# Two-layer cross attention on one core: TensorE's order inside a unit

## What is computed

```python
# layer 0
a = layer_norm(ctx);  Q, K, V = x @ Wq.T, a @ Wk.T, a @ Wv.T
attn = softmax(Q K^T / 4);  x1 = x + tanh(gate) * (attn V) @ Wo.T
# layer 1
q = layer_norm(x1) @ q_w + q_b;  k, v = ctx @ k_w + k_b, ctx @ v_w + v_b
hidden = softmax(q k^T / 4) v @ cproj_w + cproj_b + x1
y = gelu(layer_norm(hidden) @ fc_w + fc_b) @ proj_w + proj_b
return hidden + y
```

## Time and profile before

| what | us |
|---|---|
| median of 3 runs | 1924.65 |
| lowest and highest | 1922.05, 1927.8 |
| the profiled execution, its own time | 1921.35 |
| its span in the trace | 1919.6 |
| TensorE matmul busy | 1795.8 (94%) |
| TensorE weight load busy | 1172.1 (61%) |
| VectorE busy | 1405.2 (73%) |
| ScalarE busy | 1247.4 (65%) |
| GpSimd busy | 484.8 (25%) |

### The profile page before, as it was taken

The page is one execution under the profiler, slowest core; times in us unless marked ns, Lnnn a source line. Parts: engine busy times, 40 slices in busy tenths (PEclk is TensorE's granted clock), DMA queues, the critical chain, the costliest instruction groups (busy, mean ns, idle before and its releaser), DMA issues.

```text
span 1919.6 us, 83118 instructions
## 1 busy us (share of the span) xinstructions
PE 1795.8 (94%) x37316; PEld 1172.1 (61%) x37316; DVE 1405.2 (73%) x2389; ACT 1247.4 (65%) x2271; POOL 484.8 (25%) x498
## 2 busy tenths in 40 slices
PE   6789999999999999999899998999999999999996
PEld 5346656666676657666576665766666565766653
DVE  4577787777778777787767877787777877788752
ACT  3057667776567665777666776677666766576773
POOL 2041024103341043411423123420334104311130
PEclk9699999999999999999999999999999999999998
DMA  7534344252413533143431534325251353324200
GB/s 183 98 86 114 99 127 98 85 137 61 127 46 92 129 101 94 55 107 98 126 87 48 129 95 119 77 77 147 64 128 45 92 129 101 95 50 122 48 3 12
DMA packets 149785, 178.88 MB, mean 93 GB/s; under 512 B 35860, under 2 KB 113853, under 8 KB 149429
## 3 DMA queue, kind: packets, MB, share of 16 engines
q1 hardware_dynamic: 147285, 170.67, 34.5%
q10 hardware_dynamic: 2144, 2.90, 0.6%
HBM read 125.33 MB, written 48.16 MB: 90 GB/s over the span
## 4 chain that ended last, share of the span: by engine, by line
PE 68%; DVE 17%; DMA 5%; ACT 4%; POOL 2%; issue 2%; SPq 2%; ACTq 0%; POOLq 0%
PE p_misc L1186 23%; PE p_mx L1186 14%; PE p_sc L1186 14%; PE p_acc L1235 13%; DVE maxes L921 8%; PE p_misc L1256 3%; DVE rest L1001 3%; ACT parts L764 2%; DMA scr_max<-max_rows 2%; DVE parts L1012 1%; DVE o_den L949 1%; DVE st L958 1%; ACT z L797 1%; SPq L516 1%; DMA ctxn<-in_ctx_dram 1%
## 5 line engine op out<-in xcount | busy, mean ns | idle before, releaser
L921 DVE TENSOR_REDUCE maxes<-p_mx 128x1 f32<-128x802 f32 x1024 | 980.2, 982 | 249.5 <-PE p_mx L1186 245.3
L819 ACT ACTIVATE prob<-p_sc 128x512 f32<-128x512 f32 (+1 forms) x1664 | 961.1, 598 | 215.9 <-PE p_sc L1186 193.1
L1186 PE MATMUL p_sc<-qst,kst 100*32 100x256 bf16 x13056 | 705.6, 273 | 11.1 <-DMA qst<-scr_max 5.9
L1186 PE MATMUL p_mx<-kst,qst 97*32 97x401 bf16 x8192 | 580.0, 339 | 25.6 <-DVE maxes L921 24.2
L1186 PEld LDWEIGHTS p_sc<-qst,kst 100*32 100x32 bf16 x13056 | 400.2, 97 | 273.4 <-ACT prob L819 69.8
L1235 PE MATMUL p_acc<-prob,vals 128*17 128x256 f32 x6656 | 540.9, 380 | 0.3 <-ACT prob L819 0.3
L1186 PEld LDWEIGHTS p_mx<-kst,qst 97*32 97x32 bf16 x8192 | 240.7, 96 | 60.5 <-DVE maxes L921 49.7
L661 POOL TENSOR_TENSOR parts<-rest,parts 128x512 bf16<-128x512 f32 (+1 forms) x141 | 137.7, 977 | 531.1 <-DVE parts L1012 531.1
L1235 PEld LDWEIGHTS p_acc<-prob,vals 128*17 128x17 f32 x6656 | 196.3, 97 | 107.2 <-issue 64.3
L1186 PE MATMUL p_misc<-ctxt,wk 128*32 128x512 f32 (+1 forms) x1936 | 188.6, 500 | 9.4 <-ACT z L797 7.3
L1186 PE MATMUL p_misc<-wv,ctxt 128*32 128x256 f32 x3060 | 192.6, 379 | 0.0
(11 more groups left out here) (152 smaller groups left out, 1135.5 us busy)
## 6 DMA issues: line engine op xcount, KB each, us to landing
kst<-scr_k SPq DMA_DIRECT2D x384, 200.1 KB
scr_k<-parts SPq DMA_DIRECT2D x95, 384.0 KB, 3.4
ctxn<-in_ctx_dram SPq DMA_DIRECT2D x64, 384.0 KB
qst<-scr_q SPq DMA_DIRECT2D x384, 32.0 KB, 2.8
scr_q<-parts SPq DMA_DIRECT2D x15, 384.0 KB, 3.1
xin<-in_x_dram SPq DMA_DIRECT2D x8, 256.0 KB, 2.7
out_dram<-y SPq DMA_DIRECT2D x8, 256.0 KB, 2.0
scr_k<-parts SPq DMA_DIRECT2D x31, 48.8 KB, 2.4
```

Of the source, the lines that this page charges most:

```text
L819: act.activation(prob[0:rows, u % 2, 2 * half:2 * half + 2, :].rearrange("p h t -> p (h t)"), p_sc[0:rows, half, :], ACT.Exp).then_inc(exp ...
L921: dve.tensor_reduce(maxes[:, c:c + 1], p_mx[:, c % 2, :, 0:CW], AX.XY, ALU.max).then_inc(chunk_done, 1)
L1186: ins = mm(into[r0:r1, :], weights[:, r0:r1], moving, start=start, stop=stop)
```

## The change

In a unit the order on TensorE becomes: first scores, MX piece if any, second scores, first chunk, other piece, weigh, second chunk if any. No instruction is added or taken away, and the queues of the other engines stay as they were; VectorE still reduces both chunks of a unit before it reads the unit's piece.

```diff
                         scores(blk, u, 0)
                         if piece and piece[0] == "MX":
                             do_piece(blk, piece)
+                        scores(blk, u, 1)
                         if cs:
                             chunk(blk, *cs[0])
-                        scores(blk, u, 1)
-                        if len(cs) > 1:
-                            chunk(blk, *cs[1])
                         if piece and piece[0] != "MX":
                             do_piece(blk, piece)
...
                             weigh(blk.par, UNITS * blk.n + u - 1, blk.group((u - 1) // NT), u - 1,
                                   blk.n0 == 0 and u == 1)
+                        if len(cs) > 1:
+                            chunk(blk, *cs[1])
```

## The result

The changed kernel took 2031.92 us (median, 2028.75 to 2035.11), the kernel before 1925.23 beside it: a ratio of 1.0538, 95% interval 1.0512 to 1.0564, 107 us slower. The profiled execution took 2028.75 us, its span is 2027.0.

What follows compares the result with a forecast made beforehand. TensorE's queue was taken as the bound, waiting only some 14 us of 229 per pair of blocks. The profiled 1921.35 us plus 20 and 68 gave 2009, or 2013 on the median's scale; range 1959 to 2055.

Steps and rivals of the forecast that it cites:

- Part 1: Second scores ahead of the chunk: TensorE stops for ScalarE's last exponential behind plain units, 20 us (0 to 66).
- unit 8: Transposes wait for VectorE's WO read, late behind unit 7's second chunk: 1.8 us in even blocks, 1.7 in odd.
- Part 2: Second chunk behind piece and weigh in a block's 12 doubles: VectorE reads pieces late, 68 us (34 to 85).
- unit 16: TensorE loss from the late second chunk of unit 15 in even blocks, 1.3 us, and unit 14 in odd, 0.8.
- unit 18: TensorE loss from the late second chunk of unit 17 in even blocks: 0.6 us.
- unit 35: Even blocks: its MX piece starts late because unit 33's second chunk delays VectorE's read of the K piece: 1.6 us.
- unit 6: TensorE loss from the late second chunk of unit 5 in odd blocks: 0.7 us.
- unit 45: Odd blocks: its V piece starts late because unit 44's second chunk delays VectorE's read of the PJ piece: 1.3 us.
- Unit 25: Odd blocks: the second chunk no longer waits 0.82 us for the reduction before the last; gain counted as 0.25 us.
- Only part 1: Rival: idle VectorE catches up before the next piece, so only the second scores' stops show; about 1955 us, chance 0.15.
- Every double costs a reduction: Rival: each double delays VectorE by a whole reduction never made up, 188 us, 2113 us; worse than 2055, chance 0.08.
- Faster: Rival: TensorE's waits for chunks vanish, giving 1900 us, or 1851 with the loader's waits too; chance 0.06.

Runs made afterwards that it cites:

- part 1 alone: Kernel before with only the second scores moved ahead of the chunks; the second chunk stays ahead of the piece: 1950.32 us, ratio 1.0102.
- short exponentials: Exponentials of one head instead of two from the third unit on: 1919.7 us in the kernel before, 1930.32 us with both score halves ahead of the chunks.
- part 2 alone: Kernel before with only the second chunk moved behind piece and weigh; first chunk still between the score halves: 2020.58 us, ratio 1.0463.
- third experiment: Changed kernel, but with the second chunk ahead of the piece again in doubles with a K, Q, WO or PJ piece: 1953.22 us, ratio 1.0114 to kernel before.

## Why the prediction was right, and where it was not

**The bound.** TensorE's queue with 14 us of waits in 229 was the right reading, as far as these runs go: no order won more than it gave back, and half of ScalarE's exponentials left out gave 0.3%. The Trainium skill's measure (Perfetto Trace Analysis, section Identifying the Most-Contended Engine), weight loads at 61%, would have allowed a large gain; none was found here, and the start-to-start sums explain why.

**Part 1**, forecast 20 us, measured 20 (part 1 alone). The size was right, the cause half right, and that the two agree so well is luck. The stops of the second scores came at the places named; they add up to some 30 us more than before, where 40 had been worked out and halved. Taking them away (short exponentials) left 11 us, so they were worth some 10. The other 10 had no term in the sum: part of them is VectorE's chain at unit 8, which starts 0.22 us later and takes longer, part may be clock, and part is open.

**Part 2**, forecast 68 us, measured 87 to 90. The term by term working held: unit 8, 1.8 and 1.7 forecast, 1.8 and 1.8 measured; unit 16, 1.3 and 0.8 against 1.2 and 0.7; unit 18, 0.6 against 0.6; unit 35, 1.6 against 1.5; unit 6, 0.7 and 0.7; unit 45, 1.3 against 1.2. The waits say the same: those of TensorE's queue for VectorE ahead of pieces grew by 70 us, from 31 to 101, and are 37 in part 1 alone and 99 in part 2 alone.

**What was missing** is the clock. The share at half clock is twice what the mean clock lacks to 1: 2 x 0.015 x 1919.6 = 58 us before, 2 x 0.028 x 2027 = 114 after. At most half of the 56 us between them, 28, is lost time, and nearly all of it is inside the blocks; that can cover the gap of 19 us between forecast and result. The forecast had the clock at 1.00 from the earlier trace rows and no price for its fall. Only one place of it, unit 17 of even blocks (6 x 1.6 = 10 us), was tested. Unit 34 of odd blocks had no term either: its stop before the FC piece grew from 1.95 to 2.24 us in most of them, and half clock followed it in four of the six blocks 3 to 13.

**Small misses.** Unit 25 gained 0.9, not 0.25, but later units gave most of it back. Chunks were to wait hardly any more; they wait 11.9 us on the queue, half of the earlier trace rows, and the loader waits for exponentials more than before:

```profile
PEld p_sc L1186 <- ACT prob L819: 118.5, 466, 3.8
...
PEld p_mx L1186 <- DVE maxes L921: 27.4, 61, 2.7
...
PE p_mx L1186 <- DVE maxes L921: 11.9, 18, 2.3
```

**The rivals.** "Only part 1" fell since VectorE cannot make up between a piece and the next one, 1.2 us away. "Every double costs a reduction" fell with the third experiment: doubles that ScalarE reads cost nothing.

"Faster" fell although its sign came: chunks wait 12 us less on the queue, and pieces 70 more.

Still open: which stops bring the half clock. In blocks 1 to 14 of the changed kernel each of the 16 stretches came with a stop of 1.6 us or more. Another 18 such stops brought none, nor did any of 25 stops of 0.9 to 1.6 us. That of unit 16 did so in all six blocks that have it, while those of unit 8, 1.94 us in the rows above, did so in some blocks and not in others. The kernel before shows it most plainly: the stop before the FC piece of unit 34 is 1.95 us in all six blocks 3 to 13, and half clock follows it in one. Blocks 3 and 5:

```profile
502.12 3.36 PE L1186 MATMUL p_misc<-x_t,wfc 128*32 128x256 f32 x32 [1.95 <-DVE rest L1001]
...
731.68 1.94 PE L1186 MATMUL p_misc<-x_t,wfc 128*32 128x256 f32 x32 [1.95 <-DVE rest L1001]
```

and their windows from there:

```profile
502.50:505.90 3.40, 3.40 (x40) 1.63 (x32) 1.35 (x3) 0.38 (x2) 0.19 (x1) 0.50 0.14 20
731.70:735.10 3.40, 3.09 (x65) 1.87 (x69) 1.93 (x5) 1.32 (x3) 0.31 (x1) 1.00 0.11 15
```

And the size of the clock's share, up to 28 us, is bounded, not measured, but for unit 17.

## What to carry to other kernels

When work is reordered on the engine that bounds a kernel, look at the queue that consumes it: an in-order consumer that takes the moved item before another one passes the delay on to whoever waits for that other. Work it out at each place where both meet, from the rows of one unit; the places without such a meeting cost nothing that showed here. And give the clock a term with a range, from nothing to what a slow stretch costs at every new long stop: here stops of 1.6 us and more brought half clock at some places and times and not at others, and a stop no longer than one that the kernel already had could bring it.

## What the runs showed of the hardware

TensorE's granted clock can fall to its lower level after a stop inside an otherwise full stretch, though not every like stop brings it (one in six of the 1.95 us stops of unit 34 before): after 1.74 us without a matmul, the clock was 0.51 for the next 3.4 us and a piece took 3.24 us instead of 1.73; with a stop of 0.57 at the same place it stayed at 1.00. The Trainium skill (TensorE: Matmul & The Clock Gate, Part 1) says that the clock follows how busy TensorE has lately been; these traces agree that it falls after stops and is back at 1.00 afterwards. They also show the price: 1.5 us more for the one piece that fell into the slow stretch.

Two exponentials in a row overlapped more in the changed kernel. A pair in the kernel before and one in the changed kernel (start, length of both):

```profile
804.71 1.16 ACT L819 ACTIVATE prob<-p_sc 128x512 f32<-128x512 f32 x2 [0.18 <-PE p_sc L1186]
```

```profile
848.88 1.08 ACT L819 ACTIVATE prob<-p_sc 128x512 f32<-128x512 f32 x2 [0.50 <-PE p_sc L1186]
```

One exponential takes 0.60 us in both, but the second starts 0.49 us after the first instead of 0.57 (medians of all pairs), so that ScalarE's busy time for the same exponentials fell from 961.1 to 907.3 us. That its scores are there earlier is the likely reason: in the kernel before, the 51 second exponentials whose scores had been there for 0.3 us or more started after 0.48 us too. No run tested it. It gained nothing, since ScalarE was not the bound.
